# A transformer block with window attention and routed experts: the product with V turned round, and the next row's q, k and V begun at a turn's end

## The reference

```python
# block 1, y = LN(x); 16 heads of 16 channels; each token sees 7 to its left, itself, 7 to its right
q, k, v = split(LNg1(y) @ qkv_w + qkv_b)
scores  = einsum('bld,blwd->blw', q, k[window]) / 4       # k, v are 0 beyond the ends of the row
attn    = softmax(scores, axis=-1)
out     = einsum('blw,blwd->bld', attn, v[window])
y1 = y + out @ proj_w + proj_b
x1 = x + y1 + gelu_erf(LNg2(y1) @ fc1_w + fc1_b) @ fc2_w + fc2_b      # hidden width 1024
# block 2, z = LN(x1); 8 experts, two chosen for each row by the mean of its tokens
main = gelu_tanh(z @ W1m + b1m) @ W2m + b2m
p    = softmax(mean(z) @ w_gate + b_gate); e0, e1 = the two largest, weights made to sum to 1
exp_ = sum over the two of weight * (gelu_tanh(z @ W1e[e] + b1e[e]) @ W2e[e] + b2e[e])
out  = x1 + a * main + (1 - a) * exp_                     # a = clip(alpha, 0.1, 1)
```

## Time and profile before

| what | before |
|---|---|
| median of 3 runs | 2112.08 us |
| the profiled execution | 2112.47 us, span 2110.7 us |
| PE busy | 2032.2 us, 96% of the span |
| DVE busy | 1505.3 us, 71% |
| ACT busy | 1093.2 us, 52% |
| POOL busy | 1054.5 us, 50% |
| chain that ended last | PE 64%, DVE 25%, issue 6%, POOL 3% |
| granted TensorE clock | 0.995 of full speed |

### The profile page before, as it was taken

The page is one execution under the profiler, slowest core; times in us unless marked ns, Lnnn a source line. Parts: engine busy times, 40 slices in busy tenths (PEclk is TensorE's granted clock), DMA queues, the critical chain, the costliest instruction groups (busy, mean ns, idle before and its releaser), DMA issues.

```text
span 2110.7 us, 38605 instructions
## 1 busy us (share of the span) xinstructions
PE 2032.2 (96%) x13682; PEld 1845.2 (87%) x13682; DVE 1505.3 (71%) x3311; ACT 1093.2 (52%) x1716; POOL 1054.5 (50%) x989
## 2 busy tenths in 40 slices
PE   6899999999999999999999999999999999999999
PEld 6788888888889888898888898888898888989888
DVE  7568685776867669586786857768676695867853
ACT  3355555554555455554555555545554555545544
POOL 7655454553545544455554445535455444555535
PEclk9999999999999999999999999999999999999999
DMA  3021110212102121121211102121021211212111
GB/s 113 31 55 41 51 50 26 67 50 57 42 29 64 41 66 41 41 56 31 66 41 51 50 26 68 48 57 44 29 63 41 65 41 41 56 31 65 41 51 50
DMA packets 178141, 104.41 MB, mean 49 GB/s; under 512 B 58937, under 2 KB 176926, under 8 KB 177950
## 3 DMA queue, kind: packets, MB, share of 16 engines
q1 hardware_dynamic: 177374, 101.16, 17.0%
q10 hardware_dynamic: 576, 0.79, 0.1%
HBM read 81.20 MB, written 8.39 MB: 42 GB/s over the span
## 4 chain that ended last, share of the span: by engine, by line
PE 64%; DVE 25%; issue 6%; POOL 3%; ACT 1%; DMA 0%; SPq 0%; ACTq 0%; DVEq 0%; POOLq 0%
PE psB L236 32%; PE psA L236 23%; DVE tm L615 10%; DVE hr_lo L525 4%; PE psA L951 3%; PE psA L1028 3%; DVE acc L539 2%; DVE tm L631 2%; PE psA L1054 1%; DVE smax L591 1%; DVE pr L583 1%; DVE smax L598 1%; DVE y L623 1%; DVE z_lo L555 1%; DVE st L515 1%
## 5 line engine op out<-in xcount | busy, mean ns | idle before, releaser
L525 DVE TENSOR_TENSOR hr_lo<-hf,hr_hi 128x512 fp32r<-128x512 f32 x512 | 492.2, 961 | 482.0 <-ACT hr_hi L837 479.8
L837 ACT ACTIVATE hr_hi<-hf 128x512 fp32r<-128x512 f32 x512 | 323.4, 632 | 306.3 <-PE psB L236 213.0
L420 POOL TENSOR_TENSOR wx_lo<-raw,wx_hi 128x512 fp32r<-128x512 f32 x256 | 383.9, 1500 | 21.3
L418 POOL TENSOR_SCALAR wx_hi<-raw 128x512 fp32r<-128x512 f32 x256 | 169.6, 663 | 434.2 <-PE psB L236 423.9
L833 ACT ACTIVATE hf<-psB,b1x 128x512 f32<-128x512 f32 x256 | 175.5, 686 | 245.5 <-PE psB L236 242.3
L433 POOL TENSOR_SCALAR kb<-kT,gmask 128x384 f32<-128x384 f32 x128 | 158.2, 1252 | 287.2 <-ACT kT L853 287.2
L236 PE MATMUL psB<-wx_hi,hr_hi 128*128 128x256 f32 x1024 | 288.6, 282 | 0.2
L236 PE MATMUL psB<-wx_hi,hr_lo 128*128 128x256 f32 x1024 | 287.1, 280 | 0.0
L236 PE MATMUL psB<-wx_lo,hr_hi 128*128 128x256 f32 x1024 | 287.0, 280 | 0.0
L615 DVE TENSOR_TENSOR tm<-psA,rinv 32x64 f32<-32x64 f32 x1024 | 225.6, 220 | 24.8 <-PE psA L1054 11.5
L236 PE MATMUL psB<-z_hi,wx_hi 128*128 128x512 f32 x512 | 214.7, 419 | 0.0
(11 more groups left out here) (156 smaller groups left out, 5184.3 us busy)
## 6 DMA issues: line engine op xcount, KB each, us to landing
raw<-in_L_ffn_W1e SPq DMA_DIRECT2D x256, 128.0 KB, 2.2
raw<-in_L_ffn_W2e SPq DMA_DIRECT2D x256, 128.0 KB, 2.1
out_x<-acc SPq DMA_DIRECT2D x32, 256.0 KB, 2.3
xin<-in_L_attn_x SPq DMA_DIRECT2D x15, 512.0 KB, 3.7
vb<-vs SPq DMA_DIRECT2D x32, 192.0 KB
vb<-vs SPq DMA_DIRECT2D x32, 160.0 KB
raw<-in_L_attn_fc_w SPq DMA_DIRECT2D x8, 256.0 KB, 3.1
raw<-in_L_ffn_W1m SPq DMA_DIRECT2D x4, 256.0 KB, 2.7
```

Source lines behind the costliest of these rows:

```text
L418: g.tensor_scalar(wx[0][:, s, :], raw[:, s, :], 1.0, 0.0, ALU.mult, ALU.add).then_inc(w_hi.sem, 1)
L420: g.tensor_tensor(wx[1][:, s, :], raw[:, s, :], wx[0][:, s, :].bitcast(f32), ALU.subtract).then_inc(w_lo.sem, 1)
L525: v.tensor_tensor(hr[1][:, c % 2, :], hf[:, c % 3, :], hr[0][:, c % 2, :].bitcast(f32), ALU.subtract).then_inc(h_lo.sem, 1)
L837: a.activation(hr[0][:, c % 2, :], hf[:, c % 3, :], ACT.Copy).then_inc(h_hi.sem, 1)
```

## The change

In the attention, P is divided by its sums before it is turned (`normalise`: sum, reciprocal, and a multiplication of the whole unit). A block now holds both groups of 64 channels under each other in the 96 rows of `pT` and `vb`; `vb` is the stationary operand and `pT` the moving one, so that channels come out on partitions. DVE's `attended` takes each head's piece with `hmask` in four operations of 128x256, the last three of which add to the first, into `aT` (the memory of `tm` under another view). The `trA` transposes go; `attended_high` (ACT) and `attended_low` (DVE) make `zT` from `aT`. The window DMAs are twelve of half the size.

In the order, the next row's norm 1 stands in slots 24 and 26, `tr1` and `gained_T` in slot 28, its first k and q in slot 30 with their `keys` and `query_blocks`, its first V in slot 33. Scores start in slot 0. The exps stand in slots 3 and 9 instead of 6 and 11; `turn(0)` in slot 5 instead of 7. `shortcut` stands in slot 18 instead of 20, `tr3` waits for the query blocks of the next row. The router's results use bank 3 of psA. In turn 0, the number of filler matmuls (`warm`) is 104 instead of 81.

```diff
+            def normalise(t, u):
                 th, s = u % 2, unit_scores(u)
                 v.wait_ge(exped.sem, exped.at(t, u))
                 v.tensor_reduce(smax[:, th, :], s, AX.X, ALU.add).then_inc(ssum.sem, 1)
                 v.wait_ge(ssum.sem, ssum.at(t, u))
-                v.reciprocal(rinv[:, u, :, :, :].rearrange("p t g b -> p (t g b)"), smax[:, th, :]).then_inc(rinv_s.sem, 1)
+                v.reciprocal(rinv[:, th, :], smax[:, th, :]).then_inc(rinv_s.sem, 1)
+                v.wait_ge(rinv_s.sem, rinv_s.at(t, u))
+                v.tensor_tensor(s, s, rinv[:, th, :].unsqueeze(2).to_broadcast([P, UB * G, KW]), ALU.mult).then_inc(normed.sem, 1)
+            def attended(t, u):
+                c, th = divmod(u, 2)
+                v.wait_ge(av.sem, av.at(t, 2 * u + 1))
+                if t:
+                    v.wait_ge(tr3.sem, tr3.all(t - 1))
+                src = psA[:, 2:4, :].rearrange("p h (b s q) -> p (h b) s q", s=HS, q=QB)
+                dst = aT[:, c, th * UB * QB:(th + 1) * UB * QB].rearrange("p (b q) -> p b q", q=QB)
+                for s in range(HS):
+                    if s:
+                        v.wait_ge(aT_s.sem, aT_s.at(t, HS * u + s - 1))
+                        v.scalar_tensor_tensor(dst, src[:, :, s, :], hmask[:, s:s + 1], dst, ALU.mult, ALU.add).then_inc(aT_s.sem, 1)
+                    else:
+                        v.tensor_scalar(dst, src[:, :, s, :], hmask[:, s:s + 1], None, ALU.mult).then_inc(aT_s.sem, 1)
+            def attended_low(t, c):
+                v.wait_ge(tA_hi.sem, tA_hi.at(t, c))
+                v.tensor_tensor(zT[1][:, c, LEFT:LEFT + T], aT[:, c, :], zT[0][:, c, LEFT:LEFT + T].bitcast(f32), ALU.subtract).then_inc(tA_lo.sem, 1)
...
@@ PE @@
             def turn(t, u):
-                pe.wait_ge(exped.sem, exped.at(t, u))
+                pe.wait_ge(normed.sem, normed.at(t, u))
...
             def attend(t, u):
-                        last = pe.matmul(psA[:, 2 + g, j * P:(j + 1) * P], pT[0:PK, g, j, :], vb[:, j % 2, 2 * th + j // 2, c * G + g, :], start=True, stop=True)
+                        last = pe.matmul(psA[:, 2 + h, j * P:(j + 1) * P], vb[:, j, 2 * th + h, c, :], pT[0:PK, 4 * h + j, :], start=True, stop=True)
...
-                    elif q == 15:
-                        pe.wait_ge(att.sem, att.all(t))
-                        for c in range(KD):
-                            pe.wait_ge(pT_s.sem, pT_s.at(t, 6 + c))
-                            transposes(trA, c, c)
...
+                    elif q == SPLIT + 8 and t + 1 < ROWS:
+                        pe.wait_ge(z1_s.sem, z1_s.all(t + 1))
                         for c in range(KD):
                             pe.wait_ge(gelu.sem, mc(t, KH - 2 + c) + 1)
-                            transposes(tr3, c, c)
+                            transposes(tr1, c, tn)
+                    elif q == SPLIT + 10 and t + 1 < ROWS:
+                        pe.wait_ge(t1_lo.sem, t1_lo.all(t + 1))
+                        project_qk(t + 1, 0, 1, 0)
+                        project_qk(t + 1, 0, 0, 1)
+                    elif q == NQ:
+                        pe.wait_ge(z_s.sem, z_s.all(t))
+                        if t + 1 < ROWS:
+                            pe.wait_ge(kT_s.sem, kT_s.at(t + 1, 0))
+                            pe.wait_ge(qm_even.sem, qm_even.at(t + 1, 3))
+                            pe.wait_ge(qm_odd.sem, qm_odd.at(t + 1, 3))
+                        for c in range(KD):
+                            transposes(tr3, c, tm)
+                    elif q == NQ + 1:
+                        if t + 1 < ROWS:
+                            pe.wait_ge(x2.sem, x2.all(t))
+                            values(t + 1, 0)
                         route(t)
@@ POOL @@
-                    elif q == SPLIT:
+                    elif q == 18:
                         shortcut(t)
```

397 lines of the change are left out of this document (194 added, 203 removed).

## The result

The changed kernel takes 2292.06 us (median of 4 runs, 2290.66 to 2292.91) against 2112.35 us of the kernel before (4 runs): a ratio of 1.085, 95% interval 1.0831 to 1.0869. It is slower, as forecast, but by 180 us and not by 91, and outside the range given (2110 to 2240). The profiled execution has a span of 2290.2 us against 2110.7 and a granted TensorE clock of 0.966 against 0.995. PE is busy for 92% of the span (96% before), DVE 65%, ACT 48%, POOL 48%.

A forecast was written before the change was run, and what follows sets the result against it. PE was taken to bound the kernel. Waits of 3.7, 3.7, 2.1 and 0.5 less 3.5 us gained made 6.5 a turn, +97.5 over 15; with both ends +90.7, forecast 2203 us, range 2110 to 2240.

The forecast's parts named there:

- slots 10 to 16: Multiplication and new `zT_lo` ahead of `turn(2)` and the projection, under 1 us of cover: 0.5 us wait a turn (0 to 1.5).
- slots 3 to 6: Longer chain from exps through multiplication to copies: PE waits 3.7 us a turn ahead of `turn(0)` and `scores(2)` (0 to 5.5).
- turn 0: First turn, a chain of waits: shorter in the attention, longer at its end; +0.5 us, between -8 and +5.
- slots 30 to 33: Next row's k, q and query blocks ahead of chunk 23's steps: PE waits 2.1 us a turn (0 to 3).
- the gain: `trA` with its wait, the wait ahead of `attend(3)` and small items go: 3.5 us a turn less.
- a full clock in every turn: Assumption for PE's products throughout: full-clock pace; a wait costs its idle time plus some 0.15 us.
- The last row: Last row before the pure expert turn, with no next row to prepare: 7.3 us off.
- Slots 18 to 20: Moved `shortcut` additions on POOL hold DVE's two `zT_lo`: PE waits 3.7 us ahead of the first m product (0 to 4.1).
- rival 4: POOL's operations hold every DVE operation with two SBUF inputs: 8.8 us a turn more, 2238 us; chance 0.13.
- rival 5: Projection waits for new `zT_lo` as `trA` did for `tm`: 1.0 us a turn more, about 2218 us; counted within forecast's 0.50.
- Rivals 1 to 3: All chains covered, about 2055 us, 0.12; one 3.7 us wait absent, 2148 us, 0.22; waits cancel gain within 0.2%, 0.03.
- Rival 1: All chains are covered, only the gain is left: -3.5 us a turn, about 2055 us; chance 0.12.

The follow-up runs named there:

- e3: Changed kernel with 14 unused matmuls of 512 columns put into PE's wait ahead of the first m product: 2261.77 us.
- e1: Changed kernel with the two POOL additions of `shortcut` put back into slot 20: 2201.18 us.
- e2: Kernel before, with only `shortcut` moved from slot 20 to slot 18: 2195.32 us.
- e6: Changed kernel with the next row's k and q in slot 29 and DVE's query blocks behind norm 3's statistics: 2241.38 us.
- e5: Changed kernel with ACT's first two exps in slot 2 and its unit 3 query blocks behind the copies of unit 0's turned P: 2220.61 us.
- e4: Changed kernel with POOL's two `shortcut` additions replaced by one-input operations of the same size with constants: 2220.10 us.
- e10: Changed kernel with POOL's two `shortcut` additions replaced by one-input operations taking a scalar per partition from SBUF: 2207.16 us.
- e7: Changed kernel with three DVE steps (unit 2's normalisation, second-half `zT_lo`, norm 2's second half) earlier, ahead of an `hr_lo`: 2206.43 us.
- e9: Changed kernel with the edits of e1, e5, e6 and e7, and DVE's router bias row ahead of chunk 3's `hr_lo`: 2060.25 us.
- e12: Kernel before, with only the second half of norm 2's normalisation moved ahead of chunk 17's `hr_lo` on DVE: 2103.05 us.

## Why the prediction was wrong

**The sign and most of the mechanisms were right, the size was not.** Of the missing 89 us, 38 are slow matmuls behind the first m product's wait (2.5 us in 15 turns), 21 are slots 10 to 16, 15 slots 3 to 6, 12 turn 0 and 9 slots 30 to 33; against that the gain was 6 us larger than forecast.

**The step that failed: a full clock in every turn.** The sum has all of PE's products at the pace that they have in the earlier trace rows, where the clock is full, and prices a wait at its length and some 0.15 us for starting again. The slower matmuls behind a wait are the term that was mis-sized: 0 taken, 4.1 us a turn measured. Of these, 1.6 us hide the wait ahead of `scores(2)` and belong to the chain of slots 3 to 6; 2.5 us a turn, 38 us in 15 turns, are what the clock itself cost. e3 shows it alone (30 us with the wait left in place), e1 and e2 show it with the wait. It could have been read: turn 0 of the kernel before has a granted clock of 0.93, and behind the wait that the earlier trace rows show there, the six matmuls of the second m product took 2.56 us where 1.38 is their pace. I read that stretch for the wait and nothing behind it.

**Turn 0: 0.5 us forecast, 12.9 measured.** The bookkeeping failed. The last row was credited 7.3 us for having no next row (measured 7.2: turn 15 takes 132.7 us), but turn 0 now does the next row's k, q and V beside its own, 0.8 + 2.8 + 1.5 = 5.1 us of PE work, and that was left out. Of the rest, 7.8 us, by the rows of turn 0 in the section on the result, PE's idle time has 4.1 us (23.1 in place of 19.0), in waits such as 6.2 us for the query blocks ahead of `tr3` in place of 5.0 for `tm`, and 2.5 us ahead of the projection; 3.7 us are busy time, and the 23 more fillers (5.3 us at 0.23 us each, an estimate) less `trA`'s 0.87 account for it. How they share it was not tested.

**Slots 3 to 6** (3.7, about half ahead of `turn(0)`, half ahead of `scores(2)`): 3.1 us of waits and 1.6 us of slow matmuls that hide one, so 4.7 against 3.7. The chain is as told, and so is its end: 2.5 us ahead of `turn(0)` and, at full clock, 1.7 ahead of `scores(2)` (e6); the rest are small gaps around the two. What it had too short is DVE's part: `hr_lo` took 1.12 us for 0.64 and the multiplication 1.47 for 0.98, since POOL's `wx_lo` held both. e5 removes the whole, 4.7 us a turn.

**Slots 18 to 20** (3.7): 3.65, right to 0.05, and by the mechanism named. What is new is e4 and e10: the rule of the Trainium skill's "GPSIMD Engine Reference", section "Key points" (contention for DVE operations with two SBUF inputs), agrees with the trace. The rows add a price, POOL's end plus 0.54 us, and a limit that the prediction didn't have: POOL's form with a scalar from SBUF held DVE at its start alone. This also judges **rival 4**: the multiplications and `hr_lo` are held as it says (1.47 and 1.12 us where 0.96 and 0.69 stand free), but DVE has slack at most of them. Its 2238 us lies nearest to the result, by luck: the reason that it gives isn't what the time went to.

**Slots 30 to 33** (2.1): 2.7. **Slots 10 to 16** (0.5): 1.9; the lengths were known, but I granted "under 1 us of cover" where there was none, and did not name the queue: each of these steps stood behind an `hr_lo` that waited (e7).

**The gain** (3.5): 3.9. Attended units take 2.05 us (2.0 taken), the wait ahead of `attend(3)` is gone, `trA` too, and **rival 5** (the projection waits as `trA` did) is half true at 0.75 us. **Rivals 1 to 3** are out. Rival 1's floor was near, though: e9, with nearly all chains covered, takes 2060 us, and rival 1 had 2055. In part that is luck, since some 9 us of e9's lead come from norm 2's half (e12), which rival 1 left where it was.

**The range.** It took each term's bounds but none for the price of a wait as such. With the clock's 38 us alone the sum would have been 2241, just outside the range, and with turn 0's 12 as well 2253.

## What to carry to other kernels

Price a wait of the matmul engine with the matmuls behind it: read their pitch after a wait of that length in the trace (0.43 us for 0.23 here) before pricing a new one, and give that price a wide range: behind the same 3.65 us it was 1.2 to 2.5 us a turn in four orders of much the same work. Look at what ends such a slow stretch, too: where it is a wait for another engine, as ahead of `scores(2)`, a faster clock gives nothing. When a stage is moved, put the instruction that its consumer wants soonest ahead of any that still waits on its engine, and keep it clear of a long operation that holds its engine; the five moves of e9 were worth 232 us together here and turned a change that lost 8.5% into one that gains 2.4%. And when a term is credited at one end of a pipeline, look for the same work at the other.
